# A recurrent attention and Hadamard feed-forward block on one core: whole-unit loads, transposed layer-norm statistics, outputs in other places, and tokens added by accumulating DMAs

## What is computed

```
xn = layernorm(x)
phi_q, phi_k = elu(q) + 1, elu(k) + 1          # q, k, v = xn @ W.T + b
s  = (phi_q * cumsum(phi_k * v, axis=1)) * HEAD_DIM ** -0.5 @ Wo.T + bo
u  = fwht(xn * SU_ug) / 64
h  = fwht(silu(u @ W_gate.T * ws_gate) * (u @ W_up.T * ws_up) * SU_dp) / 64
g  = silu(h @ W_down.T * ws_down)
out = x + s * g
```

## Time and profile before

| | before |
|---|---|
| time, median of 3 runs | 1316.68 us (1313.84 to 1318.09) |
| time of the profiled execution | 1323.87 us |
| its span, first to last instruction | 1322.1 us |
| PE busy | 1267.6 us (96% of the span) |
| DVE, ACT, POOL busy | 957.7, 616.8, 86.0 us |
| granted PE clock, mean over the span | 0.99 of full speed |

### The profile page before, as it was taken

One profiled execution on the slowest core, in us unless ns is written; L12 is line 12 of the kernel. 1 busy time (PEld: TensorE's weight loads), 2 busy tenths in 40 slices (PEclk: granted clock), 3 DMA queues, 4 the chain that ended last, 5 costly groups with the idle time before them and its releaser, 6 DMA issues.

```text
span 1322.1 us, 16183 instructions
## 1 busy us (share of the span) xinstructions
PE 1267.6 (96%) x5896; PEld 572.3 (43%) x5896; DVE 957.7 (72%) x1444; ACT 616.8 (47%) x910; POOL 86.0 (7%) x137
## 2 busy tenths in 40 slices
PE   5998999999999999999998899999999899999997
PEld 3543444444344444444443344444444344444443
DVE  6999999877656777767574768776773867775714
ACT  5894656431235555551324555544233555554212
POOL 1001001211000000100113101000000000000000
PEclk9999999999899999999999899999999999999999
DMA  9533553677754466644537424233634332332431
GB/s 374 206 127 120 202 201 146 224 279 250 218 225 147 144 216 240 206 177 132 219 132 281 150 105 159 100 124 94 201 141 146 127 128 98 126 128 72 128 121 70
DMA packets 66847, 220.96 MB, mean 167 GB/s; under 512 B 13136, under 2 KB 19024, under 8 KB 52048
## 3 DMA queue, kind: packets, MB, share of 16 engines
q1 hardware_dynamic: 51536, 177.98, 37.9%
q0 software_dynamic: 9648, 31.99, 7.2%
q10 hardware_dynamic: 5584, 9.96, 2.2%
HBM read 166.40 MB, written 53.50 MB: 166 GB/s over the span
## 4 chain that ended last, share of the span: by engine, by line
PE 52%; DVE 5%; DMA 3%; issue 3%; ACT 2%; POOL 1%; SPq 0%; DVEq 0%; ACTq 0%
PE bank L2307 39%; PE bank L2373 6%; PE bank L2398 3%; PE bank L2493 3%; DMA scr_m<-mean_root 1%; ACT work L1168 1%; ACT work L1171 1%; DVE work L1588 1%; DMA ring<-scr_s 1%; DVE work L1572 1%; DVE h_all L1946 1%; DMA h_all<-scr_df 0%; POOL h_all L899 0%; DMA h_all<-scr_f 0%; DVE work L1578 0%
## 5 line engine op out<-in xcount | busy, mean ns | idle before, releaser
L2307 PE MATMUL bank<-xops,ring 128*128 128x512 f16 x2772 | 608.5, 381 | 19.3 <-DVE work L1588 7.1
L2307 PEld LDWEIGHTS bank<-xops,ring 128*128 128x128 f16 x2772 | 270.6, 98 | 356.2 <-issue 20.1
L2187 PE MATMUL bank<-xops,ring 128*128 128x512 f16 x1008 | 225.1, 379 | 1.3 <-DVE ring L1744 1.3
L1151 ACT ACTIVATE work<-bank 128x512 f32<-128x512 f32 x198 | 117.8, 595 | 222.0 <-PE bank L2307 207.5
L1572 DVE TENSOR_TENSOR work<-bank,work 128x512 f32<-128x512 f32 x198 | 133.6, 687 | 112.0 <-PE bank L2307 101.4
L2493 PE MATMUL bank<-h_all,ring 128*128 128x512 f16 x768 | 169.9, 384 | 4.5 <-DMA ring<-scr_d 4.3
L2187 PEld LDWEIGHTS bank<-xops,ring 128*128 128x128 f16 x1008 | 97.9, 98 | 124.8 <-issue 8.9
L2493 PEld LDWEIGHTS bank<-h_all,ring 128*128 128x128 f16 x768 | 75.7, 99 | 98.0 <-DMA ring<-scr_d 5.3
L1198 ACT ACTIVATE h_all<-work 128x512 f16<-128x512 f32 x116 | 70.5, 624 | 60.8 <-DVE work L1615 59.0
L1624 DVE TENSOR_TENSOR h_all<-work,h_all 128x512 f16<-128x512 f32 x116 | 79.4, 688 | 7.8 <-ACT h_all L1198 6.6
L1578 DVE SCALAR_TENSOR_TENSOR work<-work 128x512 f32<-128x512 f32 x64 | 44.0, 690 | 52.3 <-ACT work L1171 52.0
(11 more groups left out here) (273 smaller groups left out, 1321.2 us busy)
## 6 DMA issues: line engine op xcount, KB each, us to landing
ring<-scr_g SPq DMA_DIRECT2D x72, 1024.0 KB, 4.8
ring<-scr_d SPq DMA_DIRECT2D x16, 1024.0 KB, 6.5
scr_g<-ring SPq DMA_DIRECT2D x22, 512.0 KB, 3.3
h_all<-in_ug_t SPq DMA_DIRECT2D x8, 1024.0 KB, 12.1
ring<-in_down_t SPq DMA_DIRECT2D x6, 1024.0 KB, 6.7
scr_g<-ring POOLq DMA_DIRECT2D x12, 512.0 KB, 5.3
work<-in_x_t SPq DMA_DIRECT2D x6, 1024.0 KB, 7.4
scr_g<-h_all POOLq DMA_DIRECT2D x12, 512.0 KB, 3.7
```

What stands on the lines that cost most here:

```text
L1151: act.activation(tile(g, j), chain_bank(g)[:, :], ACT.Copy).then_inc(copied, 1)
L2187: mm = pe.matmul(plain_bank(g, j)[:, :], at[:, s, 2 * dh + kk, r, :], xops[:, kk, xs, PLAIN_B[dh][c], :], start=(n == 0), stop=(n == len(t ...
L2307: mm = pe.matmul(to[:, :], weight_of(slot, s, b, kk), at, start=(a == 0 and m in (P1, P2, P5)), stop=(a == 5), skip_group_check=True)
```

## The change

`load_unit` moves from POOL to ACT and becomes one transfer of a whole unit instead of four; for that ACT stores the down weights in pair 0 in the layout of units (`scr_u`), in four transfers for each block instead of one. All six units are now made at the end of pair 1 (before: four there, and two in groups 0 and 1 of pair 2). The first half of the next pair's token sums and the first two units move in between the tiles of the attention's output.

The means and roots are transposed by DVE in blocks of 32 by 32 before they are stored, in four transfers of 16 rows of 128 bytes. The store is split from the load: `store_stats` is issued first, other transfers follow, and only `spread_stats` waits for the landing.

In pair 2 DVE only multiplies. The tokens are no longer loaded ahead of it; POOL issues for each tile a transfer that adds them to the product in memory (`add_tokens`), and SP stores the tile once that has landed. The four late tiles of pair 2, formerly two in group 0 and two in group 1 of pair 3, are now one in group 0, one in group 1 and two in group 4.

```diff
@@
+LATE_OUTS = {0: (4,), 1: (5,), 4: (6, 7)}
+def added_by_dma(p):
+    return SEVEN_FROM <= p < PAIRS - 1
@@ sync
+            def store_stats(p):
+                sp.wait_ge(mean_root_made, p)
+                for b in range(KB):
+                    sp.dma_start(scr_m[:, 32 * b:32 * b + 32], mean_root_t[32 * b:32 * b + 4 * TB, :]) \
+                        .then_inc(mean_root_stored, 16)
             def spread_stats(p):
-                sp.wait_ge(mean_root_made, p)
-                sp.dma_start(scr_m.rearrange("m t p -> p m t"), mean_root[:, :, :], allow_slow_non_contiguous=True) \
-                    .then_inc(mean_root_stored, 16)
-                sp.wait_ge(mean_root_stored, 16 * p)
+                sp.wait_ge(mean_root_stored, 64 * p)
                 sp.dma_start(spread.rearrange("p m c n -> p (m c n)"),
...
-            def store_pair(p):
-                for n, (d, j) in enumerate(OUT_ORDER):
+            def store_pair(p, ns):
+                for n in ns:
+                    d, j = OUT_ORDER[n]
                     c, t = 2 * p + CHUNK_OF[j], d + 2 * ROW_OF[j]
-                    sp.wait_ge(out_ready, 8 * p + n + 1)
+                    if added_by_dma(p):
+                        sp.wait_ge(res_added[n % TB], 32 * (p - SEVEN_FROM) + 16 * (n // TB + 1))
+                    else:
+                        sp.wait_ge(out_ready, 8 * p + n + 1)
                     sp.dma_start(out[c, t * P:(t + 1) * P, :], res_of(c, t)).then_inc(out_stored[t], 16)
@@
                 if n == KB:
+                    store_stats(1)
+                elif n == KB + 1:
                     spread_stats(1)
@@
-                            store_pair(p - 1)
+                            store_pair(p - 1, range(6))
+                    if p > SEVEN_FROM and n == 7:
+                        store_pair(p - 1, (6, 7))
                     if n == GROUPS + (4 if p < SEVEN_FROM else 3) and p < PAIRS - 1:
+                        store_stats(p + 1)
                         load_x(p + 1)
                         spread_stats(p + 1)
@@ gpsimd
+            def add_tokens(p, n):
...
+                pool.wait_ge(out_ready, 8 * p + n + 1)
+                if p > SEVEN_FROM or n >= TB:
+                    pool.wait_ge(res_added[n % TB], 32 * (p - SEVEN_FROM) + 16 * (n // TB))
+                pool.dma_start(res_of(c, t), x_t[c, :, t, :], accum_op=ALU.add).then_inc(res_added[n % TB], 16)
@@ scalar, down_high(e)
-                act.dma_start(scr_df[e, :, :].rearrange("p (r k n) -> p r k n", r=KB, k=KB), fly_down) \
-                    .then_inc(df_stored, 16)
+                for j in range(KB):
+                    half, q0 = j // 2, 2 * (j % 2)
+                    to = scr_u[2 * q0 + e % 2:2 * q0 + 4:2, :, e // 2, half, :].rearrange("q p n -> p q n")
+                    act.dma_start(to, fly_down[:, j, :, :].rearrange("p (q k) n -> p q (k n)", q=2)).then_inc(df_stored, 16)
@@
+            def load_unit(u):
+                if u < 2:
+                    act.wait_ge(quad_done, 3 * KB)
+                    act.wait_ge(df_stored, 64 * KB)
+                else:
+                    act.wait_ge(unit_summed, u - 1)
+                act.dma_start(unit_part(u, 0).bitcast(F32), scr_u[u, :, :, :, :].rearrange("p r h n -> p r (h n)")) \
+                    .then_inc(unit_loaded[u % 2], 16)
@@ vector
-                dve.sem_inc(mean_root_made, 1)
+                dve.transpose(mean_root_t[:, :], mean_root[:, :]).then_inc(mean_root_made, 1)
@@ gated
+                if added_by_dma(p):
+                    dve.tensor_tensor(res_of(c, t), gate_of(c, t), o_of(c, t), ALU.mult).then_inc(out_ready, 1)
+                    return
@@
-                if p > SEVEN_FROM and g < 2:
-                    pair_outputs(p - 1, (4 + 2 * g, 5 + 2 * g))
-                if p == SEVEN_FROM and g < UNITS - 4:
-                    unit_add(4 + g)
-                    unit_low(3 + g)
-                    if g == UNITS - 5:
-                        unit_low(4 + g)
+                if p > SEVEN_FROM and g in LATE_OUTS:
+                    pair_outputs(p - 1, LATE_OUTS[g])
```

More of the change, by code:

```diff
@@ L260, in build @@
     scr_d = nc.dram_tensor("scr_d", (KB, P, KB, 1024), F16, kind="Internal").ap()
-    scr_df = nc.dram_tensor("scr_df", (KB, P, 2048), F32, kind="Internal").ap()
+    scr_u = nc.dram_tensor("scr_u", (FP, P, 2, 2, 256), F32, kind="Internal").ap()
     scr_s = nc.dram_tensor("scr_s", (4, P, 2, 256 * SEVEN), F16, kind="Internal").ap()
-    scr_m = nc.dram_tensor("scr_m", (2, 2 * TB, P), F32, kind="Internal").ap()
+    scr_m = nc.dram_tensor("scr_m", (4 * TB, P), F32, kind="Internal").ap()
     with ExitStack() as ctx_stack:
@@ L402, in build @@
         unit_stored = [sem(f"unit_stored{u}") for u in range(2)]
+        res_added = [sem(f"res_added{n}") for n in range(TB)]
         res_loaded = [sem(f"res_loaded{c}") for c in range(2)]
@@ L1319, in o_groups @@
                 g = GROUPS
-                for n in range(3):
-                    copy_sum(p, g, n)
+                copy_sum(p, g, 0)
+                if p < SEVEN_FROM:
+                    x_high(p + 1, 0)
+                copy_sum(p, g, 1)
+                copy_sum(p, g, 2)
                 copy_sum(p, g + 1, 0)
                 take(p, g, C21)
+                if p < SEVEN_FROM:
+                    t_high(p + 1, 0)
                 copy_sum(p, g + 1, 1)
+                if p < SEVEN_FROM:
+                    unit_high(0)
+                    load_unit(2)
                 copy_sum(p, g + 1, 2)
+                if p < SEVEN_FROM:
+                    unit_high(1)
+                    load_unit(3)
                 take(p, g + 1, C21)
```

106 lines of the change are left out of this document (54 added, 52 removed).

## The result

| | before | after |
|---|---|---|
| time, median | 1317.05 us (1313.84 to 1318.09, 4 runs) | 1304.97 us (1303.12 to 1309.63, 4 runs) |
| ratio, 95% interval | | 0.9914 (0.9890 to 0.9937) |
| profiled execution, its span | 1323.87, 1322.1 us | 1306.03, 1304.2 us |

The change gains 12.1 us; the forecast was 22.75. Faster was right, the size was not.

The account below looks back on a forecast made before the run. PE, busy 96% of the span, was taken as the bound, losing time to clustered gaps and half clock after some. Terms 5.96 + 2.02 + 13.58 - 0.97 + 2.16 = 22.75 us, off the 1316.68 median: 1293.9 us, range 1288 to 1305.

Parts of the forecast that it names:

- Statistics, 5.96 + 2.02: Quicker statistics stores remove PE's waits for `ring<-scr_d` (pair 0, with half clock) and `ring<-scr_s` (pair 2): 5.96 and 2.02 us.
- first rival: The clock doesn't come back: 8.45 us of half clock is not gained, gain 14.3, time 1302.4 us; chance 0.15.
- case 2: Start of pair 2: five PE gaps of 9.95 us together, 4.06 us of half clock, ACT idle for DVE's unit sums.
- case 4: Group 2 of pair 3: PE waits 2.86 us for DVE's `times_v`, then 1.45 us of half clock.
- cases 1 and 3: PE waits behind slow statistics stores: end of pair 0, 3.02 us plus 2.94 excess; pair 2's down projection, 2.02 us.
- Units, 13.58: Making all units at the end of pair 1 removes pair 2's starting gaps and half clock: 9.95 + 4.06 - 0.43.
- ring of loads: Rival: unit loads, sums and high parts run late ahead of the attention's output, costing 6 to 9 us; chance 0.08.
- New wait, 0.97: Attention's output of pair 1: PE's fifth product waits for a copy behind ACT's `x_high`; loss 0.97 us.
- Down weights in four transfers: Pair 0: four store issues instead of one on ACT, about 1.5 us each time, four times; costs nothing.
- slower rival: Down-weight stores in 1024 pieces of 1 KB land late in pair 0; 24 to 28 us, 1318 to 1323; chance 0.03.
- Outputs, 2.16: Pair 3: gap in group 2 falls to 0.85, group 4's work adds 1.30, half clock 1.45 goes; gain 2.16 us.
- Accumulating transfers hidden: Pair 3: added tile lands in 4.5 us, within the 6.5 allowed before group 4's weights are late; no cost.

Follow-up runs that it names:

- stats_only: The kernel before with only the transposed statistics and their split store and load; 1316.47 us, ratio 1.0001 (0.9992 to 1.0010).
- before_again: The kernel before, unchanged, profiled and timed again; 1316.74 us, ratio 0.9995 (0.9984 to 1.0005).
- units_only: The kernel before with only the units part (`scr_u`, `load_unit` on ACT, new order at the end of pair 1); 1307.38 us, ratio 0.9938.
- reordered: The changed kernel with `x_high` behind the second chain tile's copy and pair 2's late outputs in groups 0 and 3 of pair 3; 1303.06 us, ratio 0.9895.
- whole_store: The changed kernel with each block of down weights stored by one transfer in the old layout, units loaded in two; 1302.67 us, ratio 0.9895.
- other_place: The changed kernel with the scratch tensor `scr_d` declared ahead of `scr_g`, so both lie elsewhere in memory; 1305.84 us, ratio 0.9901.
- units_and_stats: The changed kernel with the outputs part (`add_tokens`, late outputs, split `store_pair`) undone; 1307.32 us, ratio 0.9926 (0.9911 to 0.9942).
- after_again: The changed kernel, unchanged, profiled and timed again; 1305.54 us, ratio 0.9917 (0.9901 to 0.9934) against the kernel before.
- units_and_outs: The changed kernel with the statistics part undone, so they are stored element by element again; 1303.41 us, ratio 0.9890 (0.9868 to 0.9911).
- plain_tokens: The changed kernel with the addition removed from `add_tokens`, so tokens overwrite the gated tiles; 1307.64 us, ratio 0.9915 (0.9890 to 0.9941).
- four_issues: The kernel whole_store with each block of down weights stored by four transfers of 2 KB pieces in the same layout; 1304.49 us, ratio 0.9895.

## Why the prediction was wrong in size

*Statistics, 5.96 + 2.02: nothing.* This is the step that failed. The stores land in 2.7 to 4.5 us, the quad goes out early, both waits are absent: all as forecast. But the kernel before has these waits only in some executions, and stats_only, which removes their cause, has a ratio of 1.0001 (0.9992 to 1.0010). The text noted that its profiled execution was 7.2 us above the median, and took "the same difference from the median". That subtracts from the median what only the outlier had. The 7.2 us are, as far as before_again shows, these waits and their clock, and the sum could have been set beside them ahead of time: 3.02 + 2.94 + 2.02 = 7.98. Against its first rival the prediction said that the gaps are in the program's order, so each run has them. That holds for case 2 and for the gap of case 4, not for the waits for landings of cases 1 and 3. Nor was the store alone to blame in case 1: 3.65 us of the quad's lateness came from DVE's wait of 5.31 us for `scr_f`.

*Units, 13.58: mechanism and size right in their place.* Gaps and half clock of 14.0 us in the first profile became waits of 0.20 to 0.32, and the walk through ACT and DVE held: no wait for units. The four profiles of the old order have 12.7 to 14.1 us there. That units_only gains only 8.2 to 9.8 of its 12.61 us fits what it loses elsewhere: 2.12 us at ACT's long issue, 1.7 of half clock behind it (92 matmuls in 21.72 us) and 0.6 more at the first quad, an estimate from single profiles. In pair 2 the clock came back where the gaps went. The first rival's 1302.4 us is nearer than my forecast, partly by luck: of its 8.45 us of half clock only the 2.94 of case 1 are missing from the ordinary execution, and the 5.0 us of waits beside them, which it kept, are missing too. Nor did the ring of loads run late.

*New wait, 0.97: 0.82 us.* It was avoidable: in reordered it is gone.

*Down weights in four transfers, nothing: up to 2.5 us.* In pair 0 the text was right. The small pieces landed in 2.2 to 3.1 us for three of the blocks, so the slower rival had no ground. It looked for the price only where the transfers stand. The price is at ACT's next burst of several issues, 260 us later, when the first takes 3.8 us and PE waits 1.53. Without it, and with a quicker first quad, whole_store is some 2.5 us faster; the profile gives 1.5 to the issue and 2.1 to the quad, less 0.7 at the attention's output, and the medians of other_place say that the quad's part is not to be counted on.

*Outputs, 2.16: 2.2 us alone* (0.8 to 3.8 by the interval), with gaps of 0.80 and 1.40 for 0.85 and 1.50. Its 1.45 us of half clock is not in every execution: units_and_stats has the gap, 2.85 us, and none behind it. *Accumulating transfers hidden:* right, there is no wait for `ring<-scr_g`.

With the two terms mended the sum is 22.75 - 7.98 - 2.5 = 12.3, and 12.1 was measured. So close an agreement is luck: the measured gain's interval is 8.3 to 14.5 us. The first of the two terms is shown by a kernel of its own; the second rests on intervals that overlap and on the rows of ACT's queue.

## What to carry to other kernels

A wait that the program's order makes was in each execution here, one that a late landing makes was in some only; a second profile of the unchanged kernel tells them apart. Where the profiled execution stands well above the median, take its surplus off the waits for landings before pricing what a change removes. Follow a transfer that is added to an engine's queue to that engine's next burst of issues, however far off. Where an engine must do extra work among a product's groups, try the groups next to it: here the same 0.65 to 1.3 us cost their full length in one and nothing in the group before it.

## What the runs showed of the hardware

- Issues on ACT's queue: the first transfer of a burst of four took 3.8 to 4.8 us to issue in every profile with 16 stores of down weights (after, after_again, units_only, units_and_stats, units_and_outs, reordered, plain_tokens, four_issues, other_place), and 0.42 or 0.43 in every one with 4. In the changed kernel the nine single loads issued in between took 0.33 or 0.34 us each. The mechanism behind it was not found.
- An accumulating transfer of 256 KB landed in 3.6 us alone, against 3.3 or 3.4 plain. Two issued 0.6 us apart ended 2.1 us apart, against 0.6 plain. The slowest of eight took 11.1 us, against 6.7.
- Transfers of 16 rows of 128 bytes, four for one set of statistics, landed in 2.7 to 4.5 us each, where 2048 elements of 4 bytes took 11.7 to 16.2 in the two profiles of the kernel before.
- The length of a wait did not settle whether half clock followed. Behind the waits for the first quad, 3.38, 3.58 and 3.68 us (reordered, after, after_again), it cost 1.7, 1.7 and 2.8 us; behind 3.75 (plain_tokens) nothing. Behind 2.86 us in pair 3 it cost 1.4 to 1.7 in four profiles, behind 2.85 (units_and_stats) nothing. Behind 2.12 (units_only) 8 matmuls took 3.05 us, 1.9 at the full clock; behind 2.22 (four_issues) 20 took 4.49, the full clock. PE's timeline of plain_tokens, then of units_and_stats:

```profile
288.49 14.85 PE L2544 MATMUL bank<-h_all,ring 128*128 128x512 f16 x68 [3.75 <-DMA ring<-scr_d]
```

```profile
1021.10 14.40 PE L2328 MATMUL bank<-xops,ring 128*128 128x512 f16 x66 [2.85 <-DVE work L1603]
```

- With another order of the scratch tensors' declarations single landings differed by up to 2.3 us, and the medians by under 1 us.
